# Both attention stages: the shift-row loads issued by ScalarE instead of the sync engine

## The reference, cut to what matters

```
q, k, v = heads of x @ W            # 16 heads x 4 batches = 64 problems of 1024 x 1024, head size 8
layer 0:  attn = softmax(q k^T + bias, causal);  out = attn v
layer 1:  alpha = softmax(q k^T / sqrt(8));  alpha = where(causal, alpha, 0);  out = alpha v
```

## Time and profile before

| | |
|---|---|
| median of three runs | 2024.98 us (2024.76 to 2026.65) |
| time of the profiled execution | 2026.05 us, its span 2024.3 us |
| busy share of the span | PE 85%, DVE 74%, ACT 66%, POOL 38% |
| causal attention, copies of `mrow` | first 146.1 us, last 553.7 us |
| full attention, copies of `mrow` | first 1270.7 us, last 1905.5 us |

### The profile page before, as it was taken

The page is one execution under the profiler, slowest core; times in us unless marked ns, Lnnn a source line. Parts: engine busy times, 40 slices in busy tenths (PEclk is TensorE's granted clock), DMA queues, the critical chain, the costliest instruction groups (busy, mean ns, idle before and its releaser), DMA issues. The chain is left out here.

```text
span 2024.3 us, 49597 instructions
## 1 busy us (share of the span) xinstructions
PE 1722.0 (85%) x19258; PEld 1066.9 (53%) x19282; DVE 1489.7 (74%) x2458; ACT 1332.7 (66%) x2543; POOL 763.9 (38%) x1506
## 2 busy tenths in 40 slices
PE   3539999999945899999989953899999999999926
PEld 1316677767634566666667731244444444444524
DVE  1759999999849545444445565999999999999445
ACT  1327888888811567766633332588888888888825
POOL 2217888888851201000000012244444444444424
PEclk9758999999965899999999976699999999999968
DMA  7342222222240000000000025111111111111031
GB/s 166 124 162 73 84 85 87 86 86 87 63 102 1 0 0 0 0 0 0 0 1 1 0 101 170 45 56 56 55 55 55 55 55 55 57 57 57 20 96 42
DMA packets 104442, 116.14 MB, mean 57 GB/s; under 512 B 21021, under 2 KB 77098, under 8 KB 104234
## 3 DMA queue, kind: packets, MB, share of 16 engines
q1 hardware_dynamic: 90410, 109.93, 17.6%
q10 hardware_dynamic: 13824, 3.34, 0.9%
HBM read 67.51 MB, written 44.59 MB: 55 GB/s over the span
## 5 line engine op out<-in xcount | busy, mean ns | idle before, releaser
L897 DVE TENSOR_REDUCE heads_mx<-heads_psM 128x1 f32<-128x1024 f32 x512 | 602.2, 1220 | 37.7 <-PE heads_psM L986 21.6
L966 ACT ACTIVATE heads_probs<-heads_psS 128x512 f32<-128x512 f32 x1024 | 546.0, 601 | 77.0 <-PE heads_psS L1009 71.0
L665 POOL TENSOR_TENSOR heads_probs<-heads_probs,one_ebias 128x256 f32<-128x256 f32 (+1 forms) x512 | 341.6, 692 | 80.2 <-ACT heads_probs L696 79.9
L935 POOL TENSOR_TENSOR heads_masked<-heads_probs,g_tri 128x128 f32<-128x128 f32 x512 | 233.9, 457 | 359.8 <-ACT heads_probs L966 359.7
L696 ACT ACTIVATE heads_probs<-heads_psS 128x512 f32<-128x512 f32 x576 | 316.3, 603 | 64.0 <-PE heads_psS L707 58.8
L629 DVE TENSOR_REDUCE heads_mx<-heads_psM 128x1 f32<-128x1024 f32 (+7 forms) x512 | 349.8, 749 | 10.3 <-PE heads_psM L707 9.6
L986 PE MATMUL heads_psM<-heads_kS,heads_qS 48*128 48x512 bf16 x1024 | 230.1, 394 | 36.5 <-DMA heads_kS<-k_parts 27.6
L1440 DVE TENSOR_TENSOR trees_hid_lo<-trees_hid,trees_hid_hi 128x512 fp32r<-128x512 f32 x192 | 139.4, 727 | 138.3 <-ACT trees_hid_hi L1424 138.3
L1009 PE MATMUL heads_psS<-heads_qS,heads_kS 50*128 50x512 bf16 x1024 | 237.7, 388 | 0.7 <-ACT heads_probs L966 0.3
L1423 ACT ACTIVATE trees_hid<-trees_psH,g_b 128x512 f32<-128x512 f32 x192 | 134.4, 700 | 112.4 <-remote 93.0
L729 PE MATMUL heads_psM<-heads_kS,heads_qS 48*128 48x512 bf16 (+3 forms) x768 | 147.7, 335 | 30.2 <-DMA heads_kS<-k_parts 27.4
(11 more groups left out here) (223 smaller groups left out, 3372.3 us busy)
## 6 DMA issues: line engine op xcount, KB each, us to landing
heads_qS<-q_parts SPq DMA_DIRECT2D x256, 96.0 KB
heads_kS<-k_parts SPq DMA_DIRECT2D x256, 96.0 KB
head_outputs<-heads_oT SPq DMA_DIRECT2D x128, 128.0 KB
q_parts<-proj_parts SPq DMA_DIRECT2D x16, 384.0 KB, 2.6
k_parts<-proj_parts SPq DMA_DIRECT2D x16, 384.0 KB, 3.3
q_parts<-proj_parts SPq DMA_DIRECT2D x16, 256.0 KB, 3.4
k_parts<-proj_parts SPq DMA_DIRECT2D x16, 256.0 KB, 3.5
heads_qS<-heads_mrow SPq DMA_DIRECT2D x256, 4.0 KB
```

The lines of the kernel that those rows point to most:

```text
L665: pool.tensor_tensor(pr[:, a:a + w], pr[:, a:a + w], g["ebias"][:, n // B, 0:w], ALU.mult).then_inc(near_done, 1)
L897: dve.tensor_reduce(mx[:, n % 2, k:k + 1], psM[k % 2][:, :], AXX, ALU.max, negate=True).then_inc(max_taken, 1)
L935: pool.tensor_tensor(masked[n % 2][:, kb, :], probs[n % 2][:, kb, kb * P:(kb + 1) * P], g["tri"][:, 0:P], ALU.mult).then_inc(near_done, 1)
L966: act.activation(probs[n % 2][:, kb, h * CH:(h + 1) * CH], ring.bank(i)[:, :], ACT.Exp).then_inc(slot_taken, 1)
```

## The change

The two DMAs of `load_shifts` leave SP's program in both stages. ACT issues them: those of step 0 right behind its copy of `mrow`, and those of step n + 1 within step n, behind the exponential of slot 4 (causal) or slot (4,0) (full). The bytes, the number of DMAs, their semaphores and the waits of all other engines stay as they were. The DMAs go out on the ring of ACT and no longer on that of SP.

```diff
-def load_shifts(sp, tile, mrow, done):
+def load_shifts(act, tile, mrow, done):

     for r in (PROWS, HALF + PROWS):
-        sp.dma_start(tile[r:r + SHIFTS, :].rearrange("s (q w) -> s q w", w=P), mrow[:, :]).then_inc(done, 16)
+        act.dma_start(tile[r:r + SHIFTS, :].rearrange("s (q w) -> s q w", w=P), mrow[:, :]).then_inc(done, 16)
...
-            def load_r(n):
-                sp.wait_ge(slot_taken, ring.rows(n) + 1)
-                load_shifts(sp, qS[n % BUFS], mrow[n % 2], r_loaded[n % BUFS])
...
             sp.wait_ge(cleared, BUFS)
-            load_r(0)
             for n in range(NG):
                 if n + 4 < NG:
                     load_s(n + 4)
                 if n >= 2:
                     store_o(n - 2)
-                if n + 1 < NG:
-                    load_r(n + 1)
...
         @block.scalar
         def _(act):
+            def load_r(n):
+                if n == 0:
+                    act.wait_ge(cleared, BUFS)
+                act.wait_ge(slot_taken, ring.rows(n) + 1)
+                load_shifts(act, qS[n % BUFS], mrow[n % 2], r_loaded[n % BUFS])
...
             take_rows(0)
+            load_r(0)
...
                     if slot == 0 and n >= 2:
                         take_o(n - 2)
+                    if slot == 4 and n + 1 < NG:
+                        load_r(n + 1)
```

More of the change, by code:

```diff
@@ L968, in _ @@
                         take_o(n - 2)
+                    if slot == (4, 0) and n + 1 < NG:
+                        load_r(n + 1)
             take_o(NG - 2)
```

## The result

The changed kernel takes 2169.89 us (median of four runs, 2161.38 to 2171.93) against 2024.87 us before: ratio 1.0703, 95% interval 1.0688 to 1.0718. That is 145 us slower. The forecast was 2089 with a range of 2059 to 2120: the right sign, but only 64 of the 145 us.

What follows compares the result with a forecast made beforehand. Both stages were taken as cycles over several engines, decided by who waits for ACT's next exponential. 2026.05 + 24 (causal) + 40 (full) = 2090 us, 2089 against the median; range 2059 to 2120.

Steps and rivals of the forecast that it cites:

- The price of a pair: ACT's time to issue the two shift DMAs, inferred from SP's issues: 1.36 us, bounds 1.27 and 1.46.
- The full stage: Exponential (4,1) 0.93 us late delays PE's score (6,0); step grows 0.65 to 10.6 us, +40 us in all.
- The causal step: Late slot 5 delays PE and POOL; step 6.78 us, +0.38 a step, +24 us in all.
- nothing measurable: Rival: ACT's issues as short as 0.40 us, a pair 0.85; about 2028 us; chance 0.06.
- faster: Rival: pair under about 0.71 us on ACT, landing waits end, causal step at its floor; 2018 us; chance 0.05.
- dearer: Rival: issue waits until the exponential ahead finishes, 0.6 us later in 124 steps; +74, 2163 us; chance 0.09.
- The landing ends the step at present: Causal stage: shift rows' landing ends today's step, but the delayed PE and POOL cycles will after the change; given nothing.
- the landing becomes the bound: Rival, causal stage: SP's q and k loads slow the landing; steps about 7.0, 2100 us; within the forecast's 0.80.
- the paragraph on what is cheap: SP's freed 1.4 us and earlier q and k loads cost and bring nothing; shift landing may come sooner.
- 0.93 late less 0.28 given back: Full stage: PE's score (6,0) 0.93 us late, about 0.28 recovered from PE's waits for DVE; step +0.65.
- the forecast's two parts: Full-stage give-back: 0.13 us at maxima behind the score pair, 0.14 at the next step's maxima; together about 0.28.
- The clock was left out of the sum: Granted clock was 1.00, the 2.4 GHz level, in both stretches, so no term was given to it.

Runs made afterwards that it cites:

- the issue alone: Kernel before, SP's shift loads kept, plus two more DMAs of the same shape issued by ACT into an unread spare tile: 2101.15 us, ratio 1.0371.
- loads held: Changed kernel, but in the causal stage SP waits for the next step's shift rows to land before loading q and k: 2157.06 us, ratio 1.0648.
- loads halved: Changed kernel, with each causal-stage q and k load cut into two DMAs of half the columns, same bytes: 2099.66 us, ratio 1.0358.
- store behind: Kernel before, with SP's causal-stage store placed behind the shift loads of the same step, nothing moved to ACT: 2018.36 us, ratio 0.9966.

## Why the prediction was wrong

**What held.** The price of a pair: 1.36 assumed, 1.28 to 1.30 measured. That the issue hides behind the exponential ahead and holds up the next one. The full stage: +40 forecast, +43 measured (in part by luck, see below). The causal step as far as the delay of the exponentials goes: 6.78 forecast; 6.74 with SP's loads left out or gone, 6.86 with the issue alone. 2026 + 21 + 43 = 2090, the forecast's sum, is within 4 us of the kernel without the loads (2094). The rivals "nothing measurable", "faster" and "dearer" all fell: ACT's issues cost what SP's cost, and the DMA does not wait for the exponential ahead. That the "dearer" rival's 2163 lies near the measured time is chance. (The "nothing measurable" rival's -8 and +9 on the median give 2026, not its 2028; nothing hangs on it.)

**What failed** is the step "The landing ends the step at present, but with the new delay the cycles above do, so I give it nothing in the sum". On ACT's ring the landing takes 2.91 us instead of 1.55 and ends the causal step again, at 7.7 us. The rival that named this, "the landing becomes the bound", had the mechanism and its place, but not its size: it took the worst waits of the trace before for a bound, a step of 7.0 and 2100 us. Those waits had been seen with the shift load in its place ahead of SP's loads on one ring, and say nothing about two rings at once.

The place of the mistake before it is the paragraph on what is cheap. Earlier loads of q and k were taken to "cost and bring nothing" because no engine waits for them. They do cost, as traffic under a small load that PE does wait for. The runs show it from both sides: no loads, 1.13 us and a step of 6.74; loads held but stores in their place, 2.56 us; neither, 6.74 again. It is not the sum of the traffic: the 16 DMA engines' busy share is 0.21 in these steps (the row of 165.00:636.00 above), less than the 0.27 before. The Trainium skill, page "DMA: Bandwidth & Descriptors", section "Queues, rings and completion order", says that an engine serves the rings in turn, packet by packet. I had read that in favour of the small load. In the packet records it cuts the other way. Alone, or in order on SP's ring, the 256 B packets mostly start 0.01 us apart (0.014 at the median in the trace before). On ACT's ring beside the loads of q and k there are stretches in which they start two at a time and 0.09 us apart, each time with 2 KB packets of 0.084 us started between; in one landing of the trace after:

```
385.20 385.29 385.39 385.48 385.57 385.67   256 B packets on ACT's ring, two at each, start in us
```

That turn-taking agrees with the page. But it is the smaller part: the first packet starts 1.07 us later than with the loads left out (2.34 against 1.27), and only 0.59 of the 1.78 us lies between the first and the last packet (1.36 against 0.77); the other 0.12 lies behind the last. What holds up the first packet isn't shown; that the engines have work of the other ring in hand when the load arrives is an argument, not a measurement. Nor is it shown that it takes a second ring: in no run do SP's loads stand less than about 0.8 us ahead of a shift load on SP's own ring. What is shown is that loads or stores issued just ahead of a shift load on ACT's ring, or beside it, make it late.

**The sizes.** Of the +98 us in the causal steps, the delay of the exponentials is (6.74 - 6.40) x 62 = 21. The long landing with the clock is (7.98 - 6.74) x 62 = 77, of which some 22 go with the eleven steps of half clock and some 55 are plain waiting. The clock was left out of the sum because it stood at 1.00 in both stages. It came down only where PE's waits for the landing had become long: in the causal windows of the kernels in which such a wait is 0.9 us at most or is gone (before, loads halved, loads left out, store behind) it is 1.00, with waits of up to 2.4 and 2.1 us (after, loads held) it is 0.95, and with the causal stage alone changed 0.97.

**A smaller miss** is hidden in the full stage, where two errors nearly cancel. The forecast was 0.93 late less 0.28 given back, 0.65. In the traces the score of (6,0) starts 1.15 us after the exponential of (4,0) before and 1.98 after: 0.83 late, since the pair of issues took 1.28 us and not 1.36. At the scores behind the next maxima (2.86 before, 3.55 after) 0.69 is left, and it stays so to the end of the step. So only about 0.15 came back, the first of the forecast's two parts (0.13); the second, in the next step's maxima, did not. The run with one issue of two shows the same 0.15 (0.18 late, 0.03 left), and with the pair behind (5,1) nothing came back.

## What to carry to other kernels

In these runs a small DMA that PE waits for was priced by what else was in flight when it landed, not only by its issue. Before a transfer is freed from an order that it "doesn't need", ask which small load will then share the engines with it, and look at the landing in a stretch of the trace where that traffic is missing. An issue on a compute engine cost how late it made the next instruction that waits for a bank; up to about 0.15 us of that was free in the full stage (one issue, 0.04 us a step), and beyond it the second issue counted in full (0.65). Where an engine in such a cycle begins to wait, look at the granted clock as well.

## What the runs showed that was not expected

The clock of TensorE fell to the 1.2 GHz level for 3.4 or 6.8 us at a time, although PE's matmuls had stood for only 1.0 to 2.1 us of a step. Of the 33 such stops of 0.9 us and more in the causal steps, eleven go with a fall: in nine it comes 0.2 to 0.9 us behind the end of the stop, in the two of 2.1 us within it. The other 22, of 0.9 to 1.3 us, have none, so stops of the same length are found on both sides. The store of a step, issued 1.7 us ahead of a shift load on the same ring, already cost the kernel before 0.4 us of landing and 8 us in all; moving one call on SP got them back.
